# The last state of each group of the scan: weighed by ScalarE and added in the bank of the turned y, instead of added by VectorE

## The chip, the cores and the metric

The kernel runs on one core of a Trainium2 chip. The metric is the time on the device in microseconds (us), the median of the runs. The core has five engines with instruction queues of their own: TensorE (PE in the profile; its weight loads are PEld), VectorE (DVE), ScalarE (ACT), GpSimd (POOL) and SyncE (SP), which issues DMAs. Each takes its instructions in order and waits for the others by semaphores. SBUF is the memory on chip, PSUM the banks that TensorE writes.

## The reference

Two layers over 2048 tokens of width 512. Layer 0 (a masked linear and a gated feed-forward with LoRA) and the second half of layer 1 (experts) aren't touched. The change is in the selective scan of layer 1, whose core is this:

```python
dt = jax.nn.softplus(ts @ W_dt.T + b_dt)
A = -jnp.exp(A_log.astype(jnp.float32))

def step(state, inp):
    dt_t, B_t, C_t, u_t = inp
    dA = jnp.exp(dt_t[..., None] * A)
    state = state * dA + (dt_t * u_t)[..., None] * B_t[:, None, :]
    y = jnp.einsum('bdn,bn->bd', state, C_t)
    return (state, y)
...
y = ys.transpose(1, 0, 2) + x * D
y = y * jax.nn.silu(gate)
return y @ W_out.T
```

1024 channels have 16 states each. y at a token is the sum over the 16 states of the state times C of that token. It is this sum, for the last of the 16 states, that the change computes in another place.

## The kernel before

Layer 1 goes over the tokens in eight chunks of 256 (`iteration(i, p, n, ...)`: i is the chunk being scanned, p the one before, whose experts are worked out meanwhile, n the next, whose inputs are prepared). The channels are cut into two groups g of four tiles of 128 (DG = 4). One step s handles one state for the four tiles of one group over all 256 tokens; a chunk has 32 steps, s = 0 to 15 for group 0 and 16 to 31 for group 1. There is no planner: the order on each engine is the order of the code, by tables of steps, and each engine's loop over the steps is written by hand.

In a step:

- GpSimd multiplies `dbu` (`db`, L2091), one tile of 128x1020; it may be AHEAD = 4 steps in front of the scan.
- ScalarE writes the decays into `ps_a` in two halves (`exps`, L1751). Half 0 of step s waits for the scan's half 0 of step s-1, half 1 for its half 1; between the halves it keeps the last column of the state before (`keep_state`, L1771, called `carry`). After `exps(s)` comes `others(s-1)`, with all the rest that ScalarE has to do.
- VectorE scans the two halves (`scans`, L2266), 128x512 each, into a ring of four states `h`.
- TensorE turns the state, eight 128x128 transposes, into the two banks of `ps_h`, one for each tile t of 128 tokens (`turn_h`, L1496).
- VectorE adds the turned state times C to `acc` (`add_state`, L2282), two operations of 128x512. In step s it handles the state of step s-1, behind the scan of s.

The first four states of a group (KC = 4) go another way: GpSimd multiplies them by C (`weigh_h(s)`, L2125, issued three steps later, after `carry` of step s), TensorE adds them up in `ps_h` (`add_h`, L1481), together with x*D (`init_acc`, L1469), and ScalarE copies the sum to `acc` (`join_acc`, L1943) at step 5 or 21 of the chunk. The first `add_state` of a group (steps 4 and 20) comes after that.

When a group is complete, TensorE turns `acc` back, two tiles of channels at a time, into the bank `ps_s` (`turn_y(i, m)`, L1506): m = 0 and 2 at steps 16 and 17 of the same chunk, m = 4 and 6 at steps 0 and 1 of the next. VectorE gates it (`make_y`, L2378), and TensorE projects y out (`out_projection`, L1520).

`add_state(15)`, the last of group 0, stands in step 16, `add_state(31)` in step 0 of the next chunk (for the last chunk behind the loop). `turn_y` for m = 0 and 4 waits for them, and so does `add_h` of the next group's first state, since it writes to the same banks of `ps_h`; `keep_c` (L1935), which overwrites C, waits for the last add of the chunk before. `ab` holds the decays of dt and later x*D; its tiles 0 to 3 are free once `init_acc` of group 0 has read them, until `dt_abs` at step 24. `h4_h` and `h4_l` hold the experts' input from steps 12 to 15 to about step 29; `variance_b` (step 9) writes there too.

## Time and profile before

| | before |
|---|---|
| median of three runs | 1515.08 us (1512.78 to 1516.43) |
| the profiled execution, time | 1514.93 us |
| the profiled execution, span | 1512.8 us |
| TensorE busy | 1352.6 us (89%) |
| VectorE busy | 1216.3 us (80%) |
| GpSimd busy | 1028.5 us (68%) |
| ScalarE busy | 951.0 us (63%) |
| scans L2266, 512 of them | 596.8 us, 1209 ns each |
| adds L2282, 384 of them | 268.7 us, 741 ns each |

The span goes from the first instruction to the last; the time of the execution includes what lies around it. Layer 0 takes roughly the first third. The eight chunks begin at about 540 us, and a chunk in the middle repeats the one before it to within 0.1 us, so that one chunk can be read for six. In the page's row of forty slices VectorE, TensorE and GpSimd all stand at 8 or 9 tenths over the scan. A record's duration contains the latency of its start and its end: on ScalarE and TensorE the next one begins before the one in front has ended. A row `x2` of the timeline merges two in a row; its duration goes from the start of the first to the end of the last. The bracket at the end gives the time that the engine was idle before it, and what ended that. The granted clock of TensorE in a middle chunk is 0.99 of full speed.

### The profile page before, as it was taken

The page shows a single profiled execution, that of the slowest core. Times are in us where ns is not written, and L with a number is a line of the kernel's source. Part 1 is how long each engine was busy: PE and PEld are TensorE (multiplying, and loading weights), DVE is VectorE, ACT ScalarE, POOL GpSimd, SP SyncE. Part 2 cuts the span into 40 slices and gives each one's busy share as a digit, 9 for nine tenths or more (in the row PEclk, how much of TensorE's full clock was granted, in tenths as well). Part 3 has the DMA queues.
Part 4 walks back from the last instruction along what each step waited for, and adds up shares of the span by engine and source line. Part 5 has one row for each costly group of instructions (what it writes and reads, how often), then busy time and mean ns, then how long its engine had stood idle before and what let it go on. Part 6 is the DMA issues. An engine that isn't in the chain of part 4 may idle for free.

```text
span 1512.8 us, 25292 instructions
## 1 busy us (share of the span) xinstructions
PE 1352.6 (89%) x8817; PEld 1009.0 (67%) x8817; DVE 1216.3 (80%) x1644; ACT 951.0 (63%) x2615; POOL 1028.5 (68%) x697
## 2 busy tenths in 40 slices
PE   6889999999999959689899899899989989988677
PEld 5567677768766748568668667667766766855543
DVE  5784664465433469999999999999999999999994
ACT  3332343233321577888888898798798887886761
POOL 0343243223211397998999899899899899899870
PEclk9699999999999979999999999999999999999689
DMA  9521222101100200100110110020030020020001
GB/s 335 190 97 51 84 84 84 56 29 36 36 29 2 91 27 1 57 29 15 57 42 1 56 58 1 22 92 1 15 99 1 15 84 15 1 71 29 1 1 42
DMA packets 32388, 77.16 MB, mean 51 GB/s; under 512 B 3667, under 2 KB 4723, under 8 KB 31750
## 3 DMA queue, kind: packets, MB, share of 16 engines
q1 hardware_dynamic: 32262, 75.55, 14.8%
q8 instruction: 70, 1.15, 0.3%
q14 instruction: 56, 0.46, 0.1%
HBM read 66.99 MB, written 8.55 MB: 50 GB/s over the span
## 4 chain that ended last, share of the span: by engine, by line
PE 32%; POOL 13%; DVE 12%; ACT 5%; issue 5%; DVEq 0%; ACTq 0%; POOLq 0%
PE ps_h L1496 10%; DVE h L2266 7%; POOL h L2125 7%; POOL dbu L2091 6%; PE ps_m L1460 4%; DVE acc L2282 3%; PE ps_o L1520 2%; ACT ps_a L1751 2%; PE ps_m L165 2%; PE ps_s L1460 2%; PE ps_m L166 2%; PE ps_m L167 2%; PE ps_m L1420 2%; ACT ab L1883 1%; PE ps_s L165 1%
## 5 line engine op out<-in xcount | busy, mean ns | idle before, releaser
L2266 DVE TENSOR_TENSOR_SCAN h<-ps_a,dbu 128x512 f32<-128x512 f32 x512 | 596.8, 1209 | 21.4 <-ACT ps_a L1751 7.1
L2091 POOL TENSOR_TENSOR dbu<-dtu,b_all 128x1020 f32<-128x1020 f32 x256 | 597.8, 2356 | 15.0 <-DVE h L2266 14.6
L1751 ACT ACTIVATE ps_a<-dt,a_neg 128x256 f32<-128x256 f32 (+1 forms) x1024 | 442.8, 466 | 68.8 <-DVE h L2266 67.7
L1496 PE MATMUL ps_h<-ident,h 128*128 128x128 f32 x1536 | 225.9, 290 | 64.2 <-DVE acc L2282 58.6
L2282 DVE SCALAR_TENSOR_TENSOR acc<-ps_h,c_cur,acc 128x512 f32<-128x512 f32 x384 | 268.7, 741 | 16.6 <-PE ps_h L1496 16.1
L1496 PEld LDWEIGHTS ps_h<-ident,h 128*128 128x128 f32 x1536 | 183.4, 149 | 120.9 <-DVE h L2266 81.8
L719 POOL TENSOR_TENSOR hid_l<-hid,hid_h 128x256 f16<-128x256 f32 (+1 forms) x88 | 77.5, 884 | 157.3 <-ACT hid_h L609 157.3
L2125 POOL TENSOR_TENSOR h<-h,c_all 128x1024 f32<-128x1024 f32 x64 | 150.8, 2356 | 18.7 <-ACT carry L1771 18.7
L601 ACT ACTIVATE sil<-ps_gu 128x256 f32<-128x256 f32 (+1 forms) x88 | 33.9, 385 | 181.4 <-PE ps_gu L167 181.4
L165 PE MATMUL ps_m<-h_h,wi_h 128*128 128x256 f16 x432 | 119.7, 277 | 2.6 <-PEq L155 2.4
L166 PE MATMUL ps_m<-h_l,wi_h 128*128 128x256 f16 x432 | 119.5, 277 | 0.0
L167 PE MATMUL ps_m<-h_h,wi_l 128*128 128x256 f16 x432 | 119.4, 276 | 0.0
L1520 PE MATMUL ps_o<-wo,y 128*128 128x512 f32 x224 | 107.3, 602 | 7.7 <-DVE x L2384 7.7
L1481 PE MATMUL ps_h<-ident,h 128*128 128x128 f32 x512 | 71.0, 285 | 36.5 <-POOL h L2125 36.5
L165 PE MATMUL ps_gu<-h_h,g_h 128*128 128x256 f16 (+1 forms) x352 | 96.6, 275 | 1.6 <-DVE u_l L1011 0.9
L1481 PEld LDWEIGHTS ps_h<-ident,h 128*128 128x128 f32 x512 | 60.7, 146 | 55.2 <-POOL h L2125 42.8
L167 PE MATMUL ps_gu<-h_h,g_l 128*128 128x256 f16 (+1 forms) x352 | 96.6, 274 | 0.0
L166 PE MATMUL ps_gu<-h_l,g_h 128*128 128x256 f16 (+1 forms) x352 | 96.6, 274 | 0.0
L165 PE MATMUL ps_gu<-h_h,u_h 128*128 128x256 f16 (+1 forms) x352 | 96.1, 273 | 0.0
L166 PE MATMUL ps_gu<-h_l,u_h 128*128 128x256 f16 (+1 forms) x352 | 96.1, 273 | 0.0
L167 PE MATMUL ps_gu<-h_h,u_l 128*128 128x256 f16 (+1 forms) x352 | 96.0, 273 | 0.0
L727 POOL COPY x<-x 128x1024 f32<-128x1024 f32 x8 | 8.3, 1037 | 120.8 <-issue 120.8
(404 smaller groups left out, 2885.6 us busy)
## 6 DMA issues: line engine op xcount, KB each, us to landing
b_all<-bt_scratch SPq DMA_DIRECT2D x32, 512.0 KB, 3.8
wm<-in_wmod SPq DMA_DIRECT2D x7, 1024.0 KB, 5.2
wo<-in_wmod SPq DMA_DIRECT2D x5, 1024.0 KB, 8.3
xa<-in_x SPq DMA_DIRECT2D x8, 512.0 KB, 4.5
stage<-in_W_in SPq DMA_DIRECT2D x4, 1024.0 KB
x_scratch<-x SPq DMA_DIRECT2D x8, 512.0 KB, 3.1
c_all<-bt_scratch SPq DMA_DIRECT2D x8, 512.0 KB, 6.1
x<-x_scratch SPq DMA_DIRECT2D x8, 512.0 KB, 3.6
```

What stands on the lines that cost most here:

```text
L165: pe.matmul(out, lh, rh, start=(first and k == 0), stop=False)
L166: pe.matmul(out, lh, rl, start=False, stop=False)
L167: mm = pe.matmul(out, ll, rh, start=False, stop=(last and k == n - 1))
L1460: pe.matmul(x_bank(m, first), diag_t[:, m, tap], xw[:, m % 2, tap:tap + CH], start=(tap == 0), stop=False)
L1481: tr = pe.matmul(ps_h[:, t, j * P:(j + 1) * P], h[:, s % RING, j, t * P:(t + 1) * P], W["ident"][:], is_transpose=True, start=(begin and j ...
L1496: tr = pe.transpose(ps_h[:, t, j * P:(j + 1) * P], h[:, s % RING, j, t * P:(t + 1) * P], W["ident"][:])
L1520: mm = pe.matmul(ps_o[:], y[:, k, tok], W["wo"][:, k], start=(k == 0), stop=(k == KI - 1))
L1751: ex = nc.scalar.activation(ps_a[:, j, j % 2:], dt[:, m, j % 2:], ACT.Exp, scale=a_neg[:, m, st:st + 1])
L2091: nc.gpsimd.tensor_tensor(dbu[:, s % AHEAD, :, 1:], dtu[:, :, 1:], b_all[:, st, 1:].unsqueeze(1).to_broadcast([P, DG, CH - 1]), ALU.mult). ...
L2125: nc.gpsimd.tensor_tensor(h[:, s % RING], h[:, s % RING], c_all[:, s % NS, :].unsqueeze(1).to_broadcast([P, DG, CH]), ALU.mult).then_inc(S ...
L2266: nc.vector.tensor_tensor_scan(h[:, s % RING, two].rearrange("p j t -> p (j t)"), ps_a[:, two].rearrange("p j t -> p (j t)"), dbu[:, s % A ...
L2282: op = nc.vector.scalar_tensor_tensor(part, ps_h[:, t], c_t, part, ALU.mult, ALU.add)
```

## The change

`add_state` of the last state of each group is gone: 2 tiles x 2 groups x 8 chunks. In its place ScalarE copies the turned state out of PSUM with the scale C, one value per partition, into `last_of[g][t]` (`weigh_last_state`). That is the memory of `ab` tiles 0 to 3 for group 0, and of `h4_h` and `h4_l` for group 1. For group 0 it stands in `others(15)`, behind `exps(16)` and in front of all else there; for group 1 at step 0 of the next chunk, behind `exps(0)`, and behind the loop for the last chunk. `turn_y` turns `acc` into `ps_s` as before, now without closing the sum in the bank, and then turns the weighed state onto it: four transposes more in each call. Waits follow: `turn_y` waits for the add of the last but one state, then, ahead of the new transposes, for `last_weighed`; `add_h` of a group's first state waits for `last_weighed`; `dt_abs` and `variance_b` wait until `turn_y` has read what they overwrite. To make room, several semaphores are merged into one each (`met`, `inv_a`, `inv_b`); the instructions that count them keep their places and their sequence.

The core of the diff:

```diff
@@ in block.tensor, add_h
                 if begin and not (first and s == 0):
-                    pe.wait_ge(S["hT_used"], added_at(i, s - 1, t) if s else added_at(i - 1, STEPS - 1, t))
+                    pe.wait_ge(S["last_weighed"], last_weighed_at(i, 0, t) if s else last_weighed_at(i - 1, NDG - 1, t))
@@ in block.tensor, turn_y
             take_s(S["y_done"], value(i, KI // 2, m // 2))
             if m % DG == 0:
-                pe.wait_ge(S["hT_used"], added_at(i, NS - 1 if m == 0 else STEPS - 1, TT - 1))
+                pe.wait_ge(S["hT_used"], added_at(i, NS - 2 if m == 0 else STEPS - 2, TT - 1))
             for j in range(2):
                 for t in range(TT):
-                    tr = pe.transpose(ps_s[:, j * CH + t * P:j * CH + (t + 1) * P], acc[:, t, (m + j) * P:(m + j + 1) * P], W["ident"][:])
+                    pe.matmul(ps_s[:, j * CH + t * P:j * CH + (t + 1) * P], acc[:, t, (m + j) * P:(m + j + 1) * P], W["ident"][:],
+                              is_transpose=True, start=(j == 0 and t == 0), stop=False, skip_group_check=True)
+            if m % DG == 0:
+                pe.wait_ge(S["last_weighed"], last_weighed_at(i, m // DG, TT - 1))
+            for j in range(2):
+                for t in range(TT):
+                    at = (m % DG + j) * P
+                    tr = pe.matmul(ps_s[:, j * CH + t * P:j * CH + (t + 1) * P], last_of[m // DG][t][:, at:at + P], W["ident"][:],
+                                   is_transpose=True, start=False, stop=True, skip_group_check=True)
@@ in block.scalar, dt_abs, keep_c
+                act.wait_ge(S["y_mm"], value(n - 1, KI // 2, DG // 2 - 1))
...
+                act.wait_ge(S["last_weighed"], i * (NDG * TT))
@@ in block.scalar, new
+        def weigh_last_state(i, g):
+
+            act.wait_ge(S["c_done"], i + 1)
+            if g == 0:
+                act.wait_ge(S["init_done"], i * NDG + 1)
+            else:
+                act.wait_ge(S["base_mm"], i * TT)
+                act.wait_ge(S["aggr_a"], TT)
+            for t in range(TT):
+                act.wait_ge(S["hT_done"], turned_at(i, use_of_step((g + 1) * NS - 1), t))
+                nc.scalar.activation(last_of[g][t], ps_h[:, t], ACT.Copy, scale=c_cur[:, t, NS - 1:NS]).then_inc(S["last_weighed"], 1)
@@ in block.scalar, others and iteration
+            if s == NS - 1:
+                weigh_last_state(i, 0)
...
             if p is not None and s == 9:
+                act.wait_ge(S["y_mm"], value(p, KI // 2, KI // 2 - 1))
                 variance_b(p)
...
                 if s:
                     others(i, p, n, first, s - 1)
+                elif not first:
+                    weigh_last_state(i - 1, NDG - 1)
@@ in block.vector, iteration
-                elif (st == 0 or st > JOIN_AT + 2) and not (first and s == 0):
-                    add_state(i if s else i - 1, (s - 1) % STEPS)
+                elif st > JOIN_AT + 2:
+                    add_state(i, s - 1)
...
-        add_state(LASTC, STEPS - 1)
```

How the rows stand on ScalarE around step 16 of chunk 3, before: from the second half of `exps(16)` over `x_tanh`, `low` and `exps(17)` with `carry(16)` in its middle.

```order
L1751 ACTIVATE ps_a<-dt,a_neg 128x256
L1751 ACTIVATE ps_a<-dt,a_neg 128x255
L1836 ACTIVATE th<-ps_m 128x256
L1802 ACTIVATE h_l<-ps_o 128x4x128
L1751 ACTIVATE ps_a<-dt,a_neg 128x256
L1751 ACTIVATE ps_a<-dt,a_neg 128x255
L1771 ACTIVATE carry<-h 128x4
```

And in the changed kernel (its line numbers are 15 higher here), at the same place on ScalarE.

```order
L1766 ACTIVATE ps_a<-dt,a_neg 128x256
L1766 ACTIVATE ps_a<-dt,a_neg 128x255
L1964 ACTIVATE ab<-ps_h,c_cur 128x512 x2
L1851 ACTIVATE th<-ps_m 128x256
L1817 ACTIVATE h_l<-ps_o 128x4x128
L1766 ACTIVATE ps_a<-dt,a_neg 128x256
L1766 ACTIVATE ps_a<-dt,a_neg 128x255
L1786 ACTIVATE carry<-h 128x4
```

The two weighings (L1964) have come in between the decays of step 16 and everything that leads to `carry(16)`.

On TensorE at the same time, before: the transposes of state 15 (L1496), the correction of the experts' input (L1368), a convolution, then `turn_y(i, 0)`.

```order
L1496 MATMUL ps_h<-ident,h 128x128 x8
L1368 MATMUL ps_o<-h_h,minus 128x512
L1460 MATMUL ps_m<-xw,diag_t 128x256 x4
L1461 MATMUL ps_m<-sel,rows 128x256
L1506 MATMUL ps_s<-ident,acc 128x128 x4
L165 MATMUL ps_o<-ra_h,h_h 128x136
```

In the changed kernel, the same place on TensorE.

```order
L1503 MATMUL ps_h<-ident,h 128x128 x8
L1375 MATMUL ps_o<-h_h,minus 128x512
L1467 MATMUL ps_m<-xw,diag_t 128x256 x4
L1468 MATMUL ps_m<-sel,rows 128x256
L1513 MATMUL ps_s<-ident,acc 128x128 x4
L1520 MATMUL ps_s<-ident,ab 128x128 x4
L165 MATMUL ps_o<-ra_h,h_h 128x136
```

`turn_y` has its second four (L1520, read from `ab`); nothing else has moved.

On VectorE, before, from the scan of step 16 (L2266, listed under the same operation as the adds) to that of step 17.

```order
L2266 SCALAR_TENSOR_TENSOR h<-ps_a,dbu 128x512 x2
L2296 SCALAR_TENSOR_TENSOR u<-th,ps_m 128x256
L2282 SCALAR_TENSOR_TENSOR acc<-ps_h,c_cur,acc 128x512 x2
L2266 SCALAR_TENSOR_TENSOR h<-ps_a,dbu 128x512 x2
L2296 SCALAR_TENSOR_TENSOR u<-th,ps_m 128x256
```

In the changed kernel, the same place on VectorE.

```order
L2302 SCALAR_TENSOR_TENSOR h<-ps_a,dbu 128x512 x2
L2332 SCALAR_TENSOR_TENSOR u<-th,ps_m 128x256
L2302 SCALAR_TENSOR_TENSOR h<-ps_a,dbu 128x512 x2
L2332 SCALAR_TENSOR_TENSOR u<-th,ps_m 128x256
L2414 SCALAR_TENSOR_TENSOR y<-ps_s,sg 128x512
```

The two adds between the scans are gone.

## Rows read from the trace of the kernel before

**Rows 1.** Busy time per stretch, us: PE, PEld, DVE, ACT, POOL (x instructions), clock, DMA.

```profile
837.68:955.82 118.14, 108.62 (x714) 83.12 (x712) 114.33 (x144) 99.03 (x284) 110.65 (x68) 0.99 0.11 37
837.68:912.04 74.36, 65.29 (x420) 46.93 (x418) 72.43 (x91) 63.59 (x172) 73.50 (x46) 0.98 0.16 51
914.31:955.24 40.93, 40.93 (x279) 34.21 (x277) 40.09 (x51) 33.39 (x108) 34.87 (x22) 1.00 0.04 14
```

**Rows 2.** Timeline of GpSimd: start, duration, engine, line, operation, idle before. `weigh_h(16)`, two chunks.

```profile
837.68 2.35 POOL L2125 TENSOR_TENSOR h<-h,c_all 128x1024 f32<-128x1024 f32 x1 [2.51 <-ACT carry L1771]
...
955.82 2.35 POOL L2125 TENSOR_TENSOR h<-h,c_all 128x1024 f32<-128x1024 f32 x1 [2.51 <-ACT carry L1771]
```

**Rows 3.** Timeline, all engines, 911 to 915: the join of group 0.

```profile
912.09 1.09 PE L1481 MATMUL ps_h<-ident,h 128*128 128x128 f32 x8 [1.14 <-POOL h L2125]
912.84 1.08 ACT L1943 ACTIVATE acc<-ps_h 128x512 f32<-128x512 f32 x2 [1.11 <-PE ps_h L1481]
...
914.31 1.41 DVE L2282 SCALAR_TENSOR_TENSOR acc<-ps_h,c_cur,acc 128x512 f32<-128x512 f32 x2 [1.04 <-PE ps_h L1496]
```

**Rows 4.** Timeline, all engines, 952.9 to 955.6: step 16 of chunk 3.

```profile
952.91 2.34 DVE L2266 TENSOR_TENSOR_SCAN h<-ps_a,dbu 128x512 f32<-128x512 f32 x2
952.97 1.03 PE L1496 MATMUL ps_h<-ident,h 128*128 128x128 f32 x8
953.61 0.36 ACT L1836 ACTIVATE th<-ps_m 128x256 f32<-128x256 f32 x1
...
954.25 0.60 ACT L1802 ACTIVATE h_l<-ps_o 128x512 f16<-128x512 f32 x1 [0.28 <-PE ps_o L1368]
954.75 0.87 ACT L1751 ACTIVATE ps_a<-dt,a_neg 128x256 f32<-128x256 f32 x2
...
955.48 1.41 DVE L2282 SCALAR_TENSOR_TENSOR acc<-ps_h,c_cur,acc 128x512 f32<-128x512 f32 x2
955.54 0.20 ACT L1771 ACTIVATE carry<-h 128x4 f32<-128x4 f32 x1
```

**Rows 5.** Groups by line and shape, 655 to 1368: busy, mean ns, idle before.

```profile
L2282 DVE SCALAR_TENSOR_TENSOR acc<-ps_h,c_cur,acc 128x512 f32<-128x512 f32 x291 | 203.7, 742 | 10.0 <-PE ps_h L1496 9.7
L1751 ACT ACTIVATE ps_a<-dt,a_neg 128x256 f32<-128x256 f32 x386 | 181.0, 469 | 38.9 <-DVE h L2266 38.1
...
L2125 POOL TENSOR_TENSOR h<-h,c_all 128x1024 f32<-128x1024 f32 x48 | 113.3, 2360 | 15.0 <-ACT carry L1771 15.0
...
L1506 PE MATMUL ps_s<-ident,acc 128*128 128x128 f32 x96 | 14.9, 278 | 5.9 <-DVE acc L2282 5.9
...
L1836 ACT ACTIVATE th<-ps_m 128x256 f32<-128x256 f32 x36 | 13.5, 374 | 0.0
L1943 ACT ACTIVATE acc<-ps_h 128x512 f32<-128x512 f32 x24 | 13.2, 595 | 12.4 <-PE ps_h L1481 12.4
```

**Rows 6.** Timeline, all engines, 773 to 778: steps 0 and 1 of chunk 2.

```profile
773.72 1.04 PE L1496 MATMUL ps_h<-ident,h 128*128 128x128 f32 x8
...
774.74 0.87 ACT L1751 ACTIVATE ps_a<-dt,a_neg 128x256 f32<-128x256 f32 x2 [0.93 <-DVE h L2266]
...
777.65 2.35 POOL L2125 TENSOR_TENSOR h<-h,c_all 128x1024 f32<-128x1024 f32 x1
777.75 0.23 ACT L1935 ACTIVATE c_cur<-ssn 128x32 f32<-128x32 f32 x1 [0.87 <-DVE acc L2282]
```

**Rows 7.** Timeline, all engines, 597 to 601: step 16 of chunk 0.

```profile
597.84 1.03 PE L1496 MATMUL ps_h<-ident,h 128*128 128x128 f32 x8
...
600.43 0.21 ACT L1771 ACTIVATE carry<-h 128x4 f32<-128x4 f32 x1 [0.30 <-DVE h L2266]
```

**Rows 8.** Timeline of ScalarE: `carry(16)` of the last chunk.

```profile
1426.04 0.21 ACT L1771 ACTIVATE carry<-h 128x4 f32<-128x4 f32 x1 [0.30 <-DVE h L2266]
```

**Rows 9.** Timeline, all engines, 1479 to 1482: the last add and `turn_y`.

```profile
1479.88 1.41 DVE L2282 SCALAR_TENSOR_TENSOR acc<-ps_h,c_cur,acc 128x512 f32<-128x512 f32 x2 [0.15 <-PE ps_h L1496]
...
1481.44 0.63 PE L1506 MATMUL ps_s<-ident,acc 128*128 128x128 f32 x4 [1.00 <-DVE acc L2282]
```

More of the change, by code:

```diff
@@ L725, in keep_x1 @@
                 pool.wait_ge(W["x2_stored"], n * 16)
-            pool.sem_inc(W["met_pool"], 1)
+            pool.sem_inc(W["met"], 1)
             nc.gpsimd.tensor_copy(x1r[:], x1[:]).then_inc(S["x1r_done"], 1)
@@ L1177, in layer_1 @@
              "du_done dt_mm dt_abs dt_exp dt_ln dt_done dtu_done c_done "
-             "exp_half b0_done dbu_done decay0_done fold_done scan_half carry_done hT_done hT_used joined init_done hc_done hc_used c_in "
+             "exp_half b0_done dbu_done decay0_done fold_done scan_half carry_done hT_done hT_used last_weighed joined init_done hc_done hc_used c_in "
              "y_mm y_done wo_mm x3_done t4_mm t4_hi t4_lo ra_mm rl_done "
@@ L1191, in layer_1, with last_weighed_at @@
     USES = NDG * (NS - KC + 1)
-    ADDS = NDG * (NS - KC)
+    ADDS = NDG * (NS - KC - 1)
     def add_of_step(s):
-        return (s // NS) * (NS - KC) + s % NS - KC
+        return (s // NS) * (NS - KC - 1) + s % NS - KC
     def added_at(i, s, t):
         return (i * ADDS + add_of_step(s)) * TT + (t + 1)
+    def last_weighed_at(i, g, t):
+        return (i * NDG + g) * TT + (t + 1)
+    last_t = (ab[:, 0:DG].rearrange("p k t -> p (k t)")[:, 0:D], ab[:, 0:DG].rearrange("p k t -> p (k t)")[:, D:2 * D])
+    last_of = (last_t, [v[:].rearrange("p k t -> p (k t)").bitcast(F32) for v in (h4_h, h4_l)])
     def joined_at(i, g, t):
@@ L1437, in turn_ss @@
             pe.wait_ge(S["ss_in"], n + 1)
-            pe.sem_inc(W["met_pe"], 1)
+            pe.sem_inc(W["met"], 1)
             for t in range(TT):
@@ L1444, in turn_tsb @@
             take_s(S["b0_done"], n + 1)
-            pe.sem_inc(W["met_pe"], 1)
+            pe.sem_inc(W["met"], 1)
             for t in range(TT):
@@ L2070, in _ @@
         iteration(LASTC, LASTC - 1, None, False)
+        weigh_last_state(LASTC, NDG - 1)
         for t in range(TT):
@@ L2107, in first_inputs @@
             pool.wait_ge(S["b0_done"], n + 1)
-            pool.sem_inc(W["met_pool"], 1)
+            pool.sem_inc(W["met"], 1)
             steps = slice(g * NS, (g + 1) * NS)
@@ L2130, in inv_std_last, with inv_std @@
             one = slice(t, t + 1)
+            done = (LASTC + t) * 3
             pool.wait_ge(S["aggr_b"], LASTC * TT + (t + 1))
-            nc.gpsimd.tensor_tensor(veps[:, one], mv[:, t, 1:2], W["epsilon"][:, one], ALU.add).then_inc(S["veps_b"], 1)
-            pool.wait_ge(S["veps_b"], NCH + t)
-            nc.gpsimd.tensor_tensor(rstd[:, one], veps[:, one], W["mhalf"][:, one], ALU.pow).then_inc(S["rstd_b"], 1)
-            pool.wait_ge(S["rstd_b"], NCH + t)
-            nc.gpsimd.tensor_tensor(nm[:, one], mv[:, t, 0:1], rstd[:, one], ALU.mult).then_inc(S["nm_b"], 1)
-            pool.wait_ge(S["nm_b"], NCH + t)
+            nc.gpsimd.tensor_tensor(veps[:, one], mv[:, t, 1:2], W["epsilon"][:, one], ALU.add).then_inc(S["inv_b"], 1)
+            pool.wait_ge(S["inv_b"], done + 1)
+            nc.gpsimd.tensor_tensor(rstd[:, one], veps[:, one], W["mhalf"][:, one], ALU.pow).then_inc(S["inv_b"], 1)
+            pool.wait_ge(S["inv_b"], done + 2)
+            nc.gpsimd.tensor_tensor(nm[:, one], mv[:, t, 0:1], rstd[:, one], ALU.mult).then_inc(S["inv_b"], 1)
+            pool.wait_ge(S["inv_b"], done + 3)
             nc.gpsimd.tensor_tensor(nmr[:, one], nm[:, one], W["mhalf"][:, 3 * TT:3 * TT + 1], ALU.mult).then_inc(S["nmr_b"], 1)
-        def inv_std(n, aggr, var, nms, ve, rs, nm_done, nmr_done):
+        def inv_std(n, aggr, var, nms, inv, nmr_done):
             pool.wait_ge(aggr, n * TT + TT)
-            nc.gpsimd.tensor_tensor(veps[:], var[:], W["epsilon"][:], ALU.add).then_inc(ve, 1)
-            pool.wait_ge(ve, n + 1)
-            nc.gpsimd.tensor_tensor(rstd[:], veps[:], W["mhalf"][:, 0:TT], ALU.pow).then_inc(rs, 1)
-            pool.wait_ge(rs, n + 1)
-            nc.gpsimd.tensor_tensor(nm[:], nms, rstd[:], ALU.mult).then_inc(nm_done, 1)
-            pool.wait_ge(nm_done, n + 1)
+            nc.gpsimd.tensor_tensor(veps[:], var[:], W["epsilon"][:], ALU.add).then_inc(inv, 1)
+            pool.wait_ge(inv, n * 3 + 1)
+            nc.gpsimd.tensor_tensor(rstd[:], veps[:], W["mhalf"][:, 0:TT], ALU.pow).then_inc(inv, 1)
+            pool.wait_ge(inv, n * 3 + 2)
+            nc.gpsimd.tensor_tensor(nm[:], nms, rstd[:], ALU.mult).then_inc(inv, 1)
+            pool.wait_ge(inv, n * 3 + 3)
             nc.gpsimd.tensor_tensor(nmr[:], nm[:], root[:], ALU.mult).then_inc(nmr_done, 1)
@@ L2179, in weigh @@
             pool.wait_ge(S["e2_done"], p * 4 + 4)
-            pool.sem_inc(W["met_pool"], 1)
+            pool.sem_inc(W["met"], 1)
             for t in range(TT):
@@ L2348, in weigh_last @@
             dve.wait_ge(S["weigh_step"], done + 1)
-            dve.sem_inc(W["met_dve"], 1)
+            dve.sem_inc(W["met"], 1)
             for t in range(TT):
@@ L2389, in choose @@
             dve.wait_ge(S["rl_done"], p + 1)
-            dve.sem_inc(W["met_dve"], 1)
+            dve.sem_inc(W["met"], 1)
             for t in range(TT):
@@ L2478, in _ @@
             dve.wait_ge(S["stats_b"], t + 1)
-            dve.sem_inc(W["met_dve"], 1)
+            dve.sem_inc(W["met"], 1)
             nc.vector.bn_aggr(mv[:, t], stats[:, t]).then_inc(S["aggr_b"], 1)
```

18 lines of the change are left out of this document (9 added, 9 removed).

## The prediction

> **What bounds the kernel now.** I read the stretch of one steady chunk first, then the waits inside it. Between two `weigh_h(16)` VectorE is busy 114.33 of 118.14 us (97%), GpSimd 110.65, TensorE 108.62 (its records overlap), ScalarE 99.03 [rows 1]. By busy share alone VectorE bounds the scan. But a chunk has two parts with different owners, and the timeline shows them.
>
> At step 16 GpSimd sits idle for 2.51 us until ScalarE has written `carry` of that step, and starts `weigh_h(16)` at 837.68; one chunk later, at 955.82, the same wait of 2.51 us stands there again [rows 2]. From 837.68 to 912.04, the end of `weigh_h(3)` of the next chunk, GpSimd is busy 73.50 of 74.36 us [rows 1]: nothing holds it up, it is the chain itself. At 912.09 TensorE, after a wait of 1.14 us for GpSimd, turns that state; ScalarE joins it at 912.84, after 1.11 us; VectorE starts `add_state(4)` at 914.31, after 1.04 us [rows 3]. From there to 955.24, where `scans(16)` ends (952.91 + 2.33, [rows 4]), VectorE is busy 40.09 of 40.93 us [rows 1]. So the loop that sets the period is `carry(16)` -> GpSimd 74.4 us -> join 2.3 us -> VectorE 40.9 us -> `scans(16)` -> 0.6 us to the next `weigh_h(16)`: 118.2 us, the period.
>
> Now place the adds that go. `add_state(15)` starts at 955.48, behind `scans(16)` [rows 4]; `add_state(31)` stands in the code behind `scans(0)` of the next chunk. Both lie in GpSimd's part, after which VectorE waits at the join anyway. Neither is on the loop.
>
> **Removed: 32 adds on VectorE.** Two tiles x two groups x eight chunks, 742 ns each [rows 5]: 23.7 us of busy time, 2.97 us a chunk. Worth on the loop: 0; VectorE only arrives earlier at the 1.04 us wait of [rows 3], which grows. What is late next there is GpSimd, as now.
>
> **Added: 32 weighings on ScalarE.** The trace has no 128x512 copy out of PSUM with a scale per partition. The plain one is the pair at 912.84: 1.08 us for two of 595 ns, so 0.49 us from start to start [rows 3, 5]. What a scale per partition adds shows at 128x256: 469 ns for `ps_a` against 374 ns for `th` [rows 5], about 0.1 us. I take 0.58 us a piece, being nearest to the row of the same shape, and 1.15 us for the pair until the next operation starts. Lower bound 0.95 us (the scale costs nothing); upper bound 1.40 us (0.595 + 0.1, with no overlap).
>
> The pair of group 0 is issued behind `exps(16)` and ahead of `x_tanh`, `low` and `exps(17)`, in whose middle `carry(16)` is written. ScalarE is free for it at 953.61 [rows 4]. A turned tile is there 0.75 us after TensorE begins its eight transposes, by 912.09 -> 912.84 [rows 3]; here they began at 952.97 [rows 4], so 953.72. The pair then runs to 954.87; `x_tanh` takes 0.26 and `low` 0.50 us (the distances in [rows 4], without the 0.28 us of idle ahead of `low`, since what it waited for has come by then); `exps(17)` starts at 955.62 instead of 954.75. As a rule: delay = pair - 0.28 = **0.87 us**, bounds 0.67 and 1.12. `carry(16)` was written at 955.54, 0.79 us behind the start of `exps(17)` [rows 4], and moves by the same. GpSimd's wait of 2.51 us becomes 3.4 us, and the loop is longer by 0.87 us. `scans(17)` could start a little earlier than before, which ends in the same wait at the join.
>
> Chunks 1 to 6 have this pattern; their six waits ahead of `weigh_h(16)` add up to 15.0 us, 2.5 each [rows 5]. That is 6 x 0.87 = 5.2 us. In chunk 0 the transposes of step 15 began at 597.84, so the pair runs 598.59 to 599.74, `x_tanh` to 600.00, and `carry(16)` comes at 600.79 instead of 600.43 [rows 7], where it had waited 0.30 us for the scan: +0.35 us. In the last chunk `carry(16)` also waits 0.30 us for the scan [rows 8]: 1.15 - 0.30 = 0.85 us.
>
> The pair of group 1 stands at the next chunk's step 0, between `exps(0)` and `exps(1)`, where ScalarE waits 0.93 us before 774.74. The transposes began at 773.72, so the pair runs 774.47 to 775.62 and `exps(1)` starts 0.9 us late [rows 6]. That is covered: `carry(0)`, 0.8 us into `exps(1)`, comes at about 776.4, and GpSimd takes `weigh_h(0)` only at 777.65. The 0.87 us that `keep_c` waited for VectorE before 777.75 [rows 6] go, so from there ScalarE is level again. Cost 0. Were the cover of 1.2 us gone, up to 0.9 us a chunk would be added.
>
> **Added: 128 transposes on TensorE**, sixteen a chunk. Eight take 1.03 us, four 0.63 [rows 4, 9]: 0.10 us for each more, 1.6 us a chunk, half at steps 16 and 17, half at the next steps 0 and 1. At step 16 TensorE waited for `add_state(15)`, 5.9 us in six chunks [rows 5]; now it waits for `last_weighed` at about 955, already past, and the 0.8 us hide in that. At steps 0 and 1 the gate tile, the out projection and `add_h(0)` are queued behind them; the 0.8 us end in TensorE's wait of 1.14 us for GpSimd [rows 3]. Cost 0. The distance of 0.10 us speaks against a rule of the Trainium skill (TensorE: Matmul & The Clock Gate, Part 4: PE-mode transpose), which gives about 275 ns for a 128x128 transpose inside a kernel: as a duration the trace agrees (278 ns, [rows 5]), as the price of one more in a queue it doesn't. By that page, as an estimate, TensorE would pay 4.4 us a chunk.
>
> **Waits and names.** `dt_abs`, `variance_b` and `keep_c` on ScalarE get waits for `y_mm` or `last_weighed`, which were reached steps earlier; `exps` and their readers queue behind them unhurt: 0. Fewer semaphores, with the same order on each engine: 0.
>
> **The end.** After the last scans `add_state(31)` ran 1479.88 to 1481.27, and TensorE turned y from 1481.44 [rows 9]. Now ScalarE's pair starts at about 1479.9 and its second ends near 1481.2: equal within 0.1. The first `turn_y` has its half from `acc` done while it waits; the second, also four transposes longer, delays the projection by 0.4 us: +0.35 us.
>
> **Sum.** 5.2 + 0.35 + 0.85 + 0.35 = +6.7 us. The profiled execution took 1514.93 us (span 1512.8) and the median of the runs is 1515.08: 1515.0 + 6.7 = **1521.7 us**. With the pair at 0.95 us: 4.0 + 0.15 + 0.65 + 0 = 4.8, 1519.8. At 1.40: 6.7 + 0.6 + 1.1 + 0.6 = 9.0, 1524.0. With the spread of the runs (1512.78 to 1516.43), the case's own range is 1518.3 to 1525.5.
>
> **Rivals.** (1) VectorE is the bound after all: it is 97% busy, and in GpSimd's part it has few gaps either (72.43 of 74.36 us, [rows 1]). Then 23.7 us are saved: 1491 us. Against it: the joins at which VectorE waits for GpSimd's chain, and that chain without a gap. The Trainium skill (Perfetto Trace Analysis, Identifying the Most-Contended Engine) has the engine with the highest occupancy relieved first, and so speaks for this rival; the busy shares agree with it, the waits don't. Chance 0.08, and 0.04 for a smaller gain (1500 to 1512).
> (2) The pair hides: the state is turned earlier than 953.72, or GpSimd takes the delay up in small gaps. Then only the end moves: 1514 to 1518 us. For it: 0.28 us of idle; against it: ScalarE has no other gap from `exps(16)` to `carry(16)`. Chance 0.18.
> (3) TensorE makes it slower still: if the eight transposes at steps 0 and 1 cost their durations (8 x 0.278 = 2.2 us), they exceed the 1.14 us it waits at 912.09, the point from which it decides, and the join is 1.1 us later in seven chunks: 1529 us. Against it: the distance of 0.10 us. Chance 0.08.
> The forecast keeps 0.62.
>
> **Numbers.** Predicted 1521.7. The forecast's range and rival 2 hold 0.80; some of rival 3's side is taken in: 1513.5 to 1527. A measurement tells about 0.2%, 3 us, from no change: faster 0.12 (rival 1 and the smaller gain), same 0.18 (rival 2), slower 0.70 (the forecast and rival 3).
>
> **What would show it.** Right: a period of 119.0 us between two `weigh_h(16)`; 3.4 us of idle ahead of it, released by `carry`; weighings of 0.6 to 0.75 us; VectorE 24 us less busy, with its idle ahead of `add_state(4)`, `add_state(20)` and in steps 1, 2 and 17 grown by as much; GpSimd's stretch of 74 us as before. Wrong: a period of 118.1 or less, a `weigh_h(16)` that starts as early after `scans(16)` as before (0.58 us), or GpSimd waiting elsewhere between `weigh_h(16)` and `weigh_h(3)`.

## The result

Over twelve runs each the changed kernel takes 1521.08 us (1515.71 to 1525.47) and the kernel before 1513.80 us (1509.91 to 1518.10): ratio 1.0046, 95% interval 1.0036 to 1.0057. It is slower by 7.0 us by the ratio; the forecast was +6.7. The profiled execution took 1522.47 us, its span is 1520.7 us.

The page of after: engine totals, shares of the chain that ended last, and the group of `weigh_h`.

```profile
PE 1368.5 (90%) x8945; PEld 1023.8 (67%) x8945; DVE 1197.6 (79%) x1612; ACT 966.8 (64%) x2647; POOL 1028.5 (68%) x697
...
PE 29%; POOL 21%; DVE 8%; ACT 5%; issue 5%; DVEq 0%; ACTq 0%; POOLq 0%
...
L2160 POOL TENSOR_TENSOR h<-h,c_all 128x1024 f32<-128x1024 f32 x64 | 151.3, 2365 | 24.8 <-ACT carry L1786 24.8
```

VectorE lost 18.7 us of busy time (the removed adds' own records add up to some 23 us, but neighbouring records overlap) and ScalarE gained 15.8, and the kernel got slower with GpSimd exactly as busy as before. The idle time ahead of `weigh_h` is the line to look at. The timeline of GpSimd in after shows it in two chunks; the busy time per stretch (columns as in [rows 1]) shows the rest:

```profile
840.29 2.36 POOL L2160 TENSOR_TENSOR h<-h,c_all 128x1024 f32<-128x1024 f32 x1 [3.37 <-ACT carry L1786]
...
959.32 2.36 POOL L2160 TENSOR_TENSOR h<-h,c_all 128x1024 f32<-128x1024 f32 x1 [3.37 <-ACT carry L1786]
```

```profile
840.29:914.70 74.41, 66.00 (x429) 47.63 (x427) 70.47 (x88) 64.58 (x174) 73.56 (x46) 0.98 0.14 51
...
840.29:959.32 119.03, 110.19 (x731) 84.69 (x730) 112.08 (x140) 101.14 (x288) 110.70 (x68) 0.99 0.10 37
```

The period is 119.03 us where it was 118.14 [rows 1], the wait for `carry` 3.37 us where it was 2.51 [rows 2]: 0.86 us more in the wait, 0.89 in the period. GpSimd's stretch up to the join is 74.41 us where it was 74.36. Step 16 of the same chunk, TensorE and ScalarE in after, against [rows 4]:

```profile
955.61 1.04 PE L1503 MATMUL ps_h<-ident,h 128*128 128x128 f32 x8
```

```profile
956.33 1.26 ACT L1964 ACTIVATE ab<-ps_h,c_cur 128x512 f32<-128x512 f32 x2
957.49 0.38 ACT L1851 ACTIVATE th<-ps_m 128x256 f32<-128x256 f32 x1
957.75 0.61 ACT L1817 ACTIVATE h_l<-ps_o 128x512 f16<-128x512 f32 x1
958.23 0.89 ACT L1766 ACTIVATE ps_a<-dt,a_neg 128x256 f32<-128x256 f32 x2
959.02 0.22 ACT L1786 ACTIVATE carry<-h 128x4 f32<-128x4 f32 x1
```

The pair starts 0.72 us behind the transposes and holds ScalarE for 1.16 us; `x_tanh`, `low` and `exps` follow without a gap, and from the transposes to `carry(16)` it is 3.41 us (955.61 to 959.02), where it was 2.57 (952.97 to 955.54, [rows 4]): +0.84.

Groups by line and shape in after, 655 to 1375 us (columns as in [rows 5]), show what the freed VectorE does:

```profile
L2318 DVE SCALAR_TENSOR_TENSOR acc<-ps_h,c_cur,acc 128x512 f32<-128x512 f32 x266 | 185.8, 737 | 14.4 <-PE ps_h L1503 13.6
...
L2414 DVE SCALAR_TENSOR_TENSOR y<-ps_s,sg 128x512 f32<-128x512 f32 x24 | 16.4, 682 | 9.0 <-PE ps_s L1520 9.0
...
L1513 PE MATMUL ps_s<-ident,acc 128*128 128x128 f32 x96 | 14.7, 276 | 0.0
...
L1964 ACT ACTIVATE ab<-ps_h,c_cur 128x512 f32<-128x512 f32 x12 | 7.6, 683 | 0.1
```

It waits. The idle time ahead of the adds went from 10.0 us [rows 5] to 14.4, and 9.0 us stand ahead of the multiplications by the gate, which had no idle time there before and now wait for the second half of `turn_y`.

The table shows where the 7.9 us between the two profiled spans lie. It is worked out from the starts of `weigh_h(16)` in the eight chunks (before 600.71, 719.37, ..., 1192.06, 1310.19; after 601.92, 721.06, ..., 1197.35, 1317.93), from the last `turn_h`, the last output projection and the span's end.

| part | before, us | after, us | difference | forecast |
|---|---|---|---|---|
| start to `weigh_h(16)` of chunk 0 | 600.71 | 601.92 | +1.21 | +0.35 |
| chunks 1 to 5 | 591.35 | 595.43 | +4.08 | +4.35 |
| chunk 6 | 118.13 | 120.58 | +2.45 | +0.87 |
| to the last `turn_h` | 169.03 | 169.96 | +0.93 | +0.85 |
| to the last projection | 4.12 | 4.45 | +0.33 | +0.35 |
| to the end | 29.46 | 28.36 | -1.10 | 0 |

The last two marks are these, TensorE in before and then in after:

```profile
1479.22 1.22 PE L1496 MATMUL ps_h<-ident,h 128*128 128x128 f32 x8 [0.46 <-DVE acc L2282]
...
1483.34 7.01 PE L1532 MATMUL ps_m<-wo,y 128*128 128x512 f32 x12
```

```profile
1487.89 1.22 PE L1503 MATMUL ps_h<-ident,h 128*128 128x128 f32 x8 [0.51 <-DVE acc L2318]
...
1492.34 7.03 PE L1547 MATMUL ps_m<-wo,y 128*128 128x512 f32 x16
```

Not all of these differences are the change's. In the first row 0.34 us are chunk 0's longer wait; the other 0.87 us arise before it, and no edit touches what the last row covers. About 1.6 us of chunk 6 go with a fall of TensorE's clock (section on hardware).

The last chunk's +0.93 us looks like the forecast 0.85 and isn't the same thing. GpSimd's wait ahead of its `weigh_h(16)` did grow by 0.70 us (1.79 to 2.49), but that instruction starts only 0.14 us later, counted from chunk 6's (116.13 us behind it before, 116.27 in after). In the kernel before, TensorE's granted clock read 0.50 at 1382 to 1384, just ahead of this chunk's first join, and the first add behind the join came 19.13 us after `weigh_h(0)` where it came after 18.51 in the changed kernel. The other 0.79 us arise behind `weigh_h(16)`. There the clock read 0.50 at 1458 to 1460 in the changed kernel, and VectorE waited twice for transposes, 0.70 us together, where it didn't in the kernel before:

```profile
1458.70 0.75 DVE L2318 SCALAR_TENSOR_TENSOR acc<-ps_h,c_cur,acc 128x512 f32<-128x512 f32 x1 [0.21 <-PE ps_h L1503]
...
1462.18 1.41 DVE L2318 SCALAR_TENSOR_TENSOR acc<-ps_h,c_cur,acc 128x512 f32<-128x512 f32 x2 [0.49 <-PE ps_h L1503]
```

### The profile page after: what moved, and what is told of

Same layout as the page of the kernel before. It is cut to its first block, busy times and chain, and to the rows that moved or that the text cites. A ratio compares the mean times of both kernels' runs of the same rounds, so it can differ in the third digit from the quotient of the medians.

```text
span 1520.7 us, 25547 instructions
## 1 busy us (share of the span) xinstructions
PE 1368.5 (90%) x8945; PEld 1023.8 (67%) x8945; DVE 1197.6 (79%) x1612; ACT 966.8 (64%) x2647; POOL 1028.5 (68%) x697
## 3 DMA queue, kind: packets, MB, share of 16 engines
q8 instruction: 71, 1.16, 0.3%
## 4 chain that ended last, share of the span: by engine, by line
PE 29%; POOL 21%; DVE 8%; ACT 5%; issue 5%; DVEq 0%; ACTq 0%; POOLq 0%
POOL dbu L2126 12%; PE ps_h L1503 9%; POOL h L2160 8%; DVE h L2302 5%; PE ps_m L1467 4%; PE ps_o L1535 3%; ACT ps_a L1766 2%; DVE acc L2318 2%; PE ps_m L165 2%; PE ps_m L166 2%; PE ps_m L167 2%; PE ps_s L1467 2%; PE ps_h L1488 1%; PE ps_m L1427 1%; PE ps_s L165 1%
## 5 line engine op out<-in xcount | busy, mean ns | idle before, releaser
L1503 PE MATMUL ps_h<-ident,h 128*128 128x128 f32 x1536 | 230.0, 293 | 61.4 <-DVE acc L2318 56.9
L2318 DVE SCALAR_TENSOR_TENSOR acc<-ps_h,c_cur,acc 128x512 f32<-128x512 f32 x352 | 245.8, 737 | 23.9 <-PE ps_h L1503 23.0
L165 PE MATMUL ps_m<-h_h,wi_h 128*128 128x256 f16 x432 | 120.2, 278 | 2.6 <-PEq L155 2.4
L166 PE MATMUL ps_m<-h_l,wi_h 128*128 128x256 f16 x432 | 120.2, 278 | 0.0
L1488 PE MATMUL ps_h<-ident,h 128*128 128x128 f32 x512 | 72.1, 286 | 49.7 <-POOL h L2160 49.7
```

The costliest lines, as they stand in the source:

```text
L165: pe.matmul(out, lh, rh, start=(first and k == 0), stop=False)
L166: pe.matmul(out, lh, rl, start=False, stop=False)
L1488: tr = pe.matmul(ps_h[:, t, j * P:(j + 1) * P], h[:, s % RING, j, t * P:(t + 1) * P], W["ident"][:], is_transpose=True, start=(begin and j ...
L1503: tr = pe.transpose(ps_h[:, t, j * P:(j + 1) * P], h[:, s % RING, j, t * P:(t + 1) * P], W["ident"][:])
L2318: op = nc.vector.scalar_tensor_tensor(part, ps_h[:, t], c_t, part, ALU.mult, ALU.add)
```

## The experiments

Each ratio is to the kernel before, timed beside it. The period is that between two `weigh_h(16)` in the middle chunks.

### The pair behind `carry(16)`

```diff
-            if s == NS - 1:
+            if s == NS:
                 weigh_last_state(i, 0)
```

> The changed kernel with one edit: ScalarE weighs the last state of group 0 in others(16), behind exps(17) and so behind carry(16), instead of in others(15). Theory (the pair of group 0 delays carry(16), which starts GpSimd's chain): the 7 us of loss go, the period between two weigh_h(16) is 118.1 us again, the ratio to the kernel before is 1.000 (within 0.999 to 1.001), and GpSimd's idle ahead of weigh_h(16) is 2.5 us. Rival (the loss comes from the new transposes on TensorE, or from the pair of group 1): the order of one pair changes nothing, ratio 1.0045.

Measured: 1512.51 us, ratio 1.0002 (0.9989 to 1.0016), period 118.3 us (118.14 before), the wait as before the change. Timelines of GpSimd and of ScalarE:

```profile
834.53 2.35 POOL L2160 TENSOR_TENSOR h<-h,c_all 128x1024 f32<-128x1024 f32 x1 [2.51 <-ACT carry L1786]
```

```profile
952.55 0.20 ACT L1786 ACTIVATE carry<-h 128x4 f32<-128x4 f32 x1
...
953.44 1.25 ACT L1964 ACTIVATE ab<-ps_h,c_cur 128x512 f32<-128x512 f32 x2
```

The same 32 weighings and 128 transposes, with `carry(16)` ahead of the pair, and the loss is gone within the interval. It was the place of two instructions in ScalarE's queue.

### Only group 0, only group 1

In each the other group keeps its add on VectorE and its plain `turn_y`.

```diff
                 elif not first:
-                    weigh_last_state(i - 1, NDG - 1)
...
-            if s == NS - 1:
-                weigh_last_state(i, 0)
```

(The first removal is that of "only group 0", the second that of "only group 1".)

> The change for group 0 alone; add_state(31) stays on VectorE, as before. Theory: all of the loss but the tail is here, 6.4 us, ratio 1.0042. Rival (the pair of group 1 at step 0, or half of the transposes each): half of the loss, ratio about 1.002, or none.

> The change for group 1 alone; add_state(15) stays on VectorE. Theory: its pair is covered by the 1.2 us between carry(0) and weigh_h(0), only the tail costs 0.35 us: ratio 1.0000 to 1.0005. Rival (the pair at step 0 costs up to 0.9 us a chunk): ratio 1.004; rival (VectorE is the bound and gains 1.4 us a chunk here): ratio 0.993.

Measured: group 0 alone 1520.34 us, ratio 1.0050 (1.0029 to 1.0071), periods of 119.0 to 119.3 us in the middle chunks (119.7 in the last of them) with 3.37 us of wait; group 1 alone 1516.45 us, 1.0019 (1.0003 to 1.0036), 118.2 us with 2.51. Group 0's pair carries all of the period's growth. Group 1 alone came out above its forecast (1.0000 to 1.0005), and its 0.19% are more than its loop explains; that stays open. Its profiled run has one chunk of 119.73 us, at whose join TensorE's granted clock read 0.82 and 0.75.

### The pair twice

```diff
             for t in range(TT):
                 act.wait_ge(S["hT_done"], turned_at(i, use_of_step((g + 1) * NS - 1), t))
+                if g == 0:
...
+                    nc.scalar.activation(relu[:, 2 * t:2 * t + 2]..., ps_h[:, t], ACT.Copy, scale=c_cur[:, t, NS - 1:NS])...
                 nc.scalar.activation(last_of[g][t], ps_h[:, t], ACT.Copy, scale=c_cur[:, t, NS - 1:NS])...
```

> The changed kernel with each of group 0's two weighings done twice (the extra one writes the same values into a buffer that is free). Dose of the suspected cost: theory, ScalarE's pair stands on the path to carry(16) and nothing covers it, so the second pair costs its whole 1.1 to 1.2 us per chunk: idle ahead of weigh_h(16) 4.5 us for 3.4, period 120.1 to 120.2 us for 119.0, 7 to 9 us more than the changed kernel, ratio to the kernel before 1.009 to 1.011. Rival (the loss comes from the waits or the order of engines, not from the pair's time): period stays at 119.0 us, ratio 1.004 to 1.005.

Measured: 1531.67 us, ratio 1.0114 (1.0096 to 1.0133), periods of 120.2 to 120.4 us, 4.57 us of wait. ScalarE and GpSimd:

```profile
961.01 0.69 ACT L1969 ACTIVATE relu<-ps_h,c_cur 128x512 f32<-128x512 f32 x1
...
963.30 0.40 ACT L1852 ACTIVATE th<-ps_m 128x256 f32<-128x256 f32 x1
```

```profile
965.15 2.35 POOL L2166 TENSOR_TENSOR h<-h,c_all 128x1024 f32<-128x1024 f32 x1 [4.58 <-ACT carry L1786]
```

Four weighings take 2.29 us (961.01 to 963.30), and the wait grew by another 1.21 us. The first pair found 0.28 us of idle to use, the second none. The price per weighing is 0.57 to 0.58 us from start to start.

### The adds left out

The last states are neither added nor weighed, and nothing is turned for them; the output lacks them.

```diff
         def weigh_last_state(i, g):
...
-            for t in range(TT):
-                act.wait_ge(...)
-                nc.scalar.activation(last_of[g][t], ps_h[:, t], ACT.Copy, scale=c_cur[:, t, NS - 1:NS])...
+            return
```

> The 32 adds of the last states are left out and nothing stands in their place: no weighing, no new transposes. y lacks the last of the sixteen states; the other work is whole. Theory (VectorE isn't the bound where those adds stood): only the tail's 1.4 us and little else are gained, 1 to 3 us, ratio 0.998 to 0.999. Rival (VectorE is the bound, 97% busy): 23.7 us less, ratio 0.984.

Measured: 1515.93 us, ratio 1.0018 (1.0003 to 1.0032), period 119.67 us in the profiled run. A miss in an unexpected direction: less work on VectorE and none added elsewhere, and in that run 1.5 us a chunk slower. VectorE is not the bound, but "no change" wasn't right either. TensorE's timeline at the join, and the stretches around it (columns as in [rows 1]):

```profile
913.79 1.10 PE L1486 MATMUL ps_h<-ident,h 128*128 128x128 f32 x8 [1.83 <-POOL h L2147]
915.29 1.94 PE L1501 MATMUL ps_h<-ident,h 128*128 128x128 f32 x8 [0.40 <-ACT acc L1959]
```

```profile
911.00:913.80 2.80, 0.97 (x9) 0.59 (x7) 2.53 (x3) 1.45 (x5) 2.80 (x3) 1.00 0.00 0
915.00:917.00 2.00, 1.71 (x8) 1.75 (x9) 0.52 (x1) 2.00 (x7) 2.00 (x2) 0.56 0.01 4
917.00:919.00 2.00, 2.00 (x5) 0.89 (x4) 1.97 (x3) 0.90 (x4) 2.00 (x2) 0.58 0.00 0
```

TensorE idles 1.83 us ahead of the join where it idled 1.14 [rows 3]; then its granted clock reads 0.56 and 0.58, about the lower of its two levels (1.2 of 2.4 GHz), for some 4 us, and eight transposes take 1.94 us instead of 1.06. Every chunk of this run from the second on shows it. But the profiled run is the slowest of the twelve (1520.07 us, 5.1 us above the kernel before's profiled run), and the ratio gives only 2.7 us: most runs can't have lost as much to it. The theory that came out of this was tested next.

### The same, with the transposes kept

```diff
-                    tr = pe.matmul(ps_s[...], last_of[m // DG][t][:, at:at + P], W["ident"][:], ...)
+                    tr = pe.matmul(ps_s[...], acc[:, t, (m + j) * P:(m + j + 1) * P], W["ident"][:], ...)
```

> The adds of the last states and their weighings are left out as in the run without the adds, but the 128 second transposes stay (they turn acc a second time, so the turned y is wrong). It asks why that run was slower than the kernel before by 1.5 us per chunk. Theory: TensorE had lost work ahead of the joins, idled 1.8 us there, and its granted clock fell to half for about 4 us; with the transposes back it idles 1.3 to 1.5 us, the clock stays up, and the period is 118.0 to 118.3 us (ratio 0.998 to 1.001). Rival (the missing adds themselves let VectorE run ahead and something else is late, whatever TensorE's clock): period 119.6 us again.

Measured: 1514.20 us, ratio 1.0003 (0.9991 to 1.0016), period 118.2 us. TensorE at the join:

```profile
905.34 1.09 PE L1486 MATMUL ps_h<-ident,h 128*128 128x128 f32 x8 [1.43 <-POOL h L2152]
906.83 1.06 PE L1501 MATMUL ps_h<-ident,h 128*128 128x128 f32 x8 [0.40 <-ACT acc L1964]
```

With the transposes back TensorE idles 1.43 us at this join, the clock stays at 1.00 there in every chunk from the second on, and the 1.5 us are gone. This rests on one profiled run of each kernel, the slowest of twelve against the fastest of twelve (1506.55 us, of which 6.9 us were gained before chunk 0's `weigh_h(16)`, where nothing was changed); the intervals of the two ratios overlap. The two runs also give the clean price of the removed adds: 32 of them gone, with no weighing in their place, are worth 0 within the interval.

### The transposes left out, the weighings kept

```diff
-            for j in range(2):
-                for t in range(TT):
...
-                    tr = pe.matmul(ps_s[...], last_of[m // DG][t][:, at:at + P], W["ident"][:], ...)
```

> The changed kernel with the weighings kept and the 128 second transposes left out (the turned y lacks each group's last state). What the transposes of TensorE cost by themselves. Theory of the prediction (they cost nothing inside the loop, only up to 0.35 us at the tail): period of the chunks 119.0 us, as with them, and 1520 to 1521 us, ratio to the kernel before 1.0043 to 1.0047. Rival (TensorE's queue sets the loop): period 118.1 to 118.5 us, 1514 to 1517 us. Second rival, from the run without the adds, where TensorE stood idle for 1.8 us ahead of the joining transposes and its granted clock then read 0.56: TensorE with less work again stands idle for longer there, the clock falls, and the period is 119.5 to 120.5 us, ratio 1.007 to 1.010.

Measured: 1518.84 us, ratio 1.0027 (1.0017 to 1.0037), periods of 119.0 to 119.5 us. The period isn't shorter without the transposes, so inside the loop they cost nothing. The clock fell at none of the middle chunks' joins of group 0, although TensorE idled 1.52 to 1.63 us there, and the period stayed at 119, so the second rival falls. (In the last chunk, with 1.78 us of idle, it did fall.) The ratio missed the expected 1.0043 to 1.0047: the whole is 2 to 3 us faster than the changed kernel, more than the 0.35 us expected. In the profiled run this lies behind the last `weigh_h(16)`: 83.3 us to the end where both kernels have 86.5. The trace tells half of it. From the last `turn_h` to the last projection it is 2.94 us (1486.69 to 1489.63), where it is 4.45 in the changed kernel and 4.12 before: without the transposes `turn_y` waits neither for a last add nor for a last weighing. So 1.5 us of the 3.2 are the last state's way into y, by whatever engine. The rest differs with TensorE's clock in the last chunk and behind it, and stays open.

### One add of dt from GpSimd to VectorE

On the kernel before, and on the one with the late pair.

```diff
-            if n is not None and s == STEPS - 3:
-                dt_add(n, 0)
...
+                if n is not None and s == STEPS - 4:
+                    dve.wait_ge(S["dt_ln"], n * 2 + 1)
+                    nc.vector.tensor_tensor(dt[:, 0:DG], dt[:, 0:DG], ab[:, 0:DG], ALU.add).then_inc(S["dt_done"], 1)
```

> The kernel before with one GpSimd instruction of each chunk, the add that finishes dt of group 0 (2.3 us), moved to VectorE behind the scans of step 28. Theory: GpSimd's stretch from weigh_h(16) to weigh_h(3) sets the loop, so it can give 2.3 us per chunk, but VectorE's stretch to scans(16) takes about 1.1 us more and has only 1 to 1.8 us of room beside GpSimd, so period 117.3 to 117.7 us for 118.14 and ratio 0.9955 to 0.998. Rival (VectorE's sum is the bound): period 119.2 us, ratio 1.004 to 1.006.

> The changed kernel with group 0's weighings behind carry(16), as in the run late, and the same add of dt moved from GpSimd to VectorE. VectorE has now lost its adds of the last states (two of 0.74 us per group), so it has the room that it lacks in the other kernel: theory, GpSimd's stretch shrinks by 2.3 us and nearly all of it shows, period 116.0 to 116.8 us, 1497 to 1503 us, ratio 0.990 to 0.993. Rival (the join's chain over TensorE, ScalarE and VectorE keeps its time whatever GpSimd does): period 117.3 to 117.8 us, as in the kernel before with the same move.

Measured: 1522.00 us, ratio 1.0048 (1.0034 to 1.0061), period 119.05 us on the kernel before; 1523.73 us, 1.0054 (1.0041 to 1.0068), and 119.2 to 120.1 us on the other. The first came out at its rival's period; the second missed both. VectorE and GpSimd of the first:

```profile
762.36 2.20 DVE L2402 TENSOR_TENSOR dt<-dt,ab 128x1024 f32<-128x1024 f32 x1
```

```profile
765.57 0.36 POOL L2101 TENSOR_TENSOR decay<-decay,carry 128x64 f32<-128x64 f32 x1 [2.09 <-ACT decay L1765]
...
779.20 2.36 POOL L2125 TENSOR_TENSOR h<-h,c_all 128x1024 f32<-128x1024 f32 x1 [0.71 <-ACT carry L1771]
```

The add takes 2.20 us here where I had put 1.1. In chunk 0 of the same run it takes 1.20; GpSimd is idle there, and here it is still at its `dbu` until 763.47:

```profile
643.38 1.20 DVE L2402 TENSOR_TENSOR dt<-dt,ab 128x1024 f32<-128x1024 f32 x1
```

```profile
756.48 6.99 POOL L2091 TENSOR_TENSOR dbu<-dtu,b_all 128x1020 f32<-128x1020 f32 x3
```

GpSimd, relieved of 2.3 us, waits 2.09 and 0.71 us for ScalarE, and ScalarE for what VectorE now delivers late. With the late pair the wait ahead of `weigh_h(0)` is up to 2.10 us: there group 1's pair stands ahead of `carry(0)`, after ScalarE has waited 1.77 us for the turned state. GpSimd's stretch without a gap is thus no proof that it alone sets the pace. On the kernel before, 2.20 us more on VectorE made the period 0.9 us longer, so as an estimate VectorE had 1.3 us of room beside GpSimd; with the late pair, 1.9 us more cost 0.9 to 1.8. Whether the add's length alone does this or also its place in VectorE's queue wasn't tested.

### Two adds less inside the other stretch

```diff
+                if s in (10, 12):
+                    part = part[:, 0:1]
+                    op = nc.vector.scalar_tensor_tensor(part, ps_h[:, t, 0:1], c_t, part, ALU.mult, ALU.add)
+                    op.then_inc(S["hT_used"], 1)
+                    continue
```

> The kernel before with the adds of states 10 and 12 cut to one column on VectorE (they are left out of y otherwise): 2 x 1.3 us of VectorE taken away per chunk, this time inside the stretch between the join and scans(16), which the prediction gave to VectorE. Theory of the prediction (VectorE sets that stretch): period down by 2.2 to 2.6 us, to 115.5 to 115.9 us, ratio 0.986 to 0.989. Rival (TensorE, which shows no gap there either, sets it, or as good as): period 117.7 to 118.2 us, ratio 0.997 to 1.0.

Measured: 1513.99 us, ratio 1.0001 (0.9991 to 1.0012), period 118.2 us. The prediction's stretch of VectorE isn't VectorE's alone. From `add_state(4)` to the end of `scans(16)`, and VectorE's timeline in it:

```profile
913.59:954.52 40.93, 40.93 (x279) 34.21 (x277) 38.26 (x51) 33.39 (x108) 34.81 (x22) 1.00 0.05 14
```

```profile
935.29 2.34 DVE L2266 TENSOR_TENSOR_SCAN h<-ps_a,dbu 128x512 f32<-128x512 f32 x2 [0.29 <-ACT carry L1771]
938.40 0.42 DVE L2301 SCALAR_TENSOR_TENSOR u<-th,ps_s 128x256 f32<-128x256 f32 x1 [0.78 <-ACT th L1836]
```

VectorE is busy 1.8 us less and the stretch is 40.93 us to the hundredth, as in [rows 1]. VectorE now waits for ScalarE, and ScalarE in its turn for TensorE:

```profile
945.05 0.20 ACT L1817 ACTIVATE xw<-hist 128x3 f32<-128x3 f32 x1 [0.80 <-PE ps_m L167]
```

TensorE is busy for all of it in both kernels; its column said so in [rows 1] and I read past it.

### Less of TensorE's work there too

```diff
-                        out_projection(p, q)
+                        if q != 5:
+                            out_projection(p, q)
```

on top of the last one, and, on the kernel with the late pair, one half of that part moved ahead of the join:

```diff
                 if s == JOIN_AT:
+                    if p is not None:
+                        out_projection(p, 5, half=0)
                     add_h(i, KC - 1, first)
```

> The same two adds cut, and TensorE's four matmuls of the output projection of step 6 (1.72 us) left out besides, ahead of the same stretch. If TensorE sets the stretch once VectorE has room: period down by up to 1.7 us against the run with the adds cut alone. If VectorE sets it: the same period as that run. Should TensorE's clock fall for lack of work, its granted clock in the stretch shows it and the period is 1.5 us longer.

> The kernel with the late weighing, with half of one output-projection part (two matmuls, 0.86 us) moved from behind the join of group 0 into TensorE's idle 1.33 us ahead of it. Theory: the join is not delayed, TensorE's queue behind the join is 0.86 us shorter, and if TensorE has a part in the stretch up to scans(16) the period falls by 0.2 to 0.9 us (117.4 to 118.1, ratio 0.993 to 0.999). Rival (VectorE sets the stretch): period 118.3 us as in the run late, ratio 1.000.

Measured: 1514.40 us, ratio 1.0003 (0.9994 to 1.0013), period 118.16 us; and 1513.45 us, 1.0001 (0.9991 to 1.0011), 118.27 us. No gain from either. TensorE of the first:

```profile
912.50 1.22 PE L1496 MATMUL ps_h<-ident,h 128*128 128x128 f32 x8 [0.56 <-DVE acc L2288]
...
916.05 1.23 PE L1496 MATMUL ps_h<-ident,h 128*128 128x128 f32 x8 [0.60 <-DVE acc L2288]
```

Both waits are for VectorE's adds. The work taken from TensorE turned into waits. The first 4.4 us behind the join, in the same run:

```profile
911.61:916.05 4.44, 3.27 (x16) 1.61 (x14) 4.44 (x6) 3.44 (x12) 4.44 (x3) 1.00 0.00 0
```

VectorE is busy for all of it, TensorE for 3.27 us. The reading that fits the three runs is two owners in turn: for 4.5 us behind the join VectorE (914.31 to 918.79 in before), then for 34.2 us TensorE's queue of transposes, convolutions and input tiles (up to 952.97, where the last transposes ahead of `carry(16)` begin). It is reached by elimination: the first experiment cut VectorE in TensorE's part, these two cut TensorE in VectorE's part. What a cut of each in its own part gives wasn't run, so it isn't shown, and no version here is faster than the kernel before.

## Why the prediction was right, step by step

**The adds are worth 0.** Right, and shown: without them and with nothing in their place, but TensorE's work kept, the period is 118.2 us and the ratio 1.0003. Rival 1 (1491 us) falls. The rule of the Trainium skill that was weighed there (Perfetto Trace Analysis, Identifying the Most-Contended Engine) picks VectorE by its busy share; here this case's runs disagree with it: 32 adds less (20.4 us of VectorE's busy time) gave nothing; cutting two adds in the stretch behind the join gave nothing either.

**The pair costs 1.15 us, less 0.28 us of idle, on the way to `carry(16)`.** Right in mechanism and size: 1.16 us for the pair, +0.84 us at `carry(16)`, +0.86 in GpSimd's wait, +0.89 in the period. Moving the pair behind `carry(16)` undoes it, doubling it adds 1.21 us. A copy out of PSUM with a scale per partition takes 683 ns, 0.09 us more than the plain one (595, [rows 5]); the estimate was 0.1 us from a smaller shape.

**Chunk 0, the last chunk and the end.** +0.34 in chunk 0's wait (2.30 for 1.96 us) and +0.33 for the end stand against 0.35 and 0.35. In the last chunk the pair's part is right (GpSimd's wait +0.70 us, 0.85 forecast), but the +0.93 us of the table are not that: 0.6 of the 0.70 are hidden by a fall of the clock in the kernel before, and 0.8 us come later with a fall in the changed one. Neither was in the prediction, and that they cancel is luck. In after the last step runs as foreseen:

```profile
1488.64 0.69 ACT L1964 ACTIVATE h_h<-ps_h,c_cur 128x512 f32<-128x512 f32 x1 [0.63 <-PE ps_h L1503]
1489.23 0.68 ACT L1964 ACTIVATE h_l<-ps_h,c_cur 128x512 f32<-128x512 f32 x1
```

**The pair of group 1 costs 0.** Right for the period: `carry(0)` was written 1.53 us ahead of `weigh_h(0)` before, and 1.06 us ahead of it with the pair in between (in the changed kernel and in the run late). The forecast left 1.2 us.

**The transposes cost 0.** Right inside the loop, against rival 3: the period is no longer with them than without. In the profiled run of the kernel without the adds they even save 1.5 us a chunk, through the clock. For the whole kernel the step isn't shown: without them it is 2 to 3 us faster, of which 1.5 us lie at the end and belong to the last state's way as much as to the transposes. The 275 ns that the Trainium skill gives for one (TensorE: Matmul & The Clock Gate, Part 4: PE-mode transpose) are its duration here too (276 ns in after), and not its price.

**The loop.** Here the prediction's account was wrong in a part on which the sum didn't rest: cutting VectorE's work in "join 2.3 us -> VectorE 40.9 us" shortened nothing, and the runs point to VectorE for 4.5 us and TensorE for the rest. Had the change removed adds in steps 8 to 15 instead, the same reading would have forecast a gain of more than 1 us per pair of adds, and missed. And GpSimd's 74 us leave VectorE only some 1.3 us of room, by the estimate above.

**The sum.** It met the measurement (+6.7 and +7.0 us) more closely than its steps deserve. The interval of the ratio alone is 5.4 to 8.6 us. In the profiled runs the steps of the forecast make 5.8 us (0.34 in chunk 0, 4.08 in chunks 1 to 5, 0.89 for chunk 6 if it is taken like its neighbours, then 0.14 and 0.33), and falls of the clock and parts that the change doesn't touch make up the rest of the 7.9. The mechanism is shown by the moved pair and the doubled pair, not by this agreement.

## What to carry to other kernels

Work moved off the busiest engine is worth only what that engine's last-ending waits say; the place that it moves to has to be read instruction by instruction in that engine's queue: here two copies of 0.58 us a chunk ahead of a small copy that another engine waits for cost 7 us in the whole, behind it nothing. Before a stretch is given to one engine, look for every column that equals the stretch: where two engines show no gap, cutting one can gain nothing.
